# When a block of the adjacency matrix may be stored: an exact count of slots in place of a constant

## The reference

```
h = relu(layernorm(x)); x = x + L0(h)   # three rounds of: tmp = tmp + segment_sum(tmp[src], dst) / deg
h = relu(layernorm(x)); x = x + L1(h)   # means of edge attributes by src and by dst, then two dense products
h = relu(layernorm(x)); x = x + L2(h)   # attention over edges: softmax of scores by dst, weighted sum
h = relu(layernorm(x)); x = x + L3(h)   # messages from node features, spherical and radial edge terms, gates
```

## Time and profile before

| | |
|---|---|
| time, median of 3 runs | 2495.79 us (2492.46 to 2499.66) |
| span of the profiled execution, first to last instruction | 2205.5 us |
| the profiled execution's own time | not recorded; the median less the span is 290.3 us |
| mean granted TensorE clock | 0.824 of 2.4 GHz |
| build of the adjacency, DVE's first visit to PE's first step of L0 | 66.35 to 344.29 us |
| visits, pairs, stores | 590, 106, 27 |

### The profile page before, as it was taken

The page is one execution under the profiler, slowest core; times in us unless marked ns, Lnnn a source line. Parts: engine busy times, 40 slices in busy tenths (PEclk is TensorE's granted clock), DMA queues, the critical chain, the costliest instruction groups (busy, mean ns, idle before and its releaser), DMA issues.

```text
span 2205.5 us, 36859 instructions
## 1 busy us (share of the span) xinstructions
PE 1640.1 (74%) x8603; PEld 1281.5 (58%) x8603; DVE 1788.0 (81%) x5309; ACT 1113.4 (50%) x2935; POOL 865.1 (39%) x861
## 2 busy tenths in 40 slices
PE   3656667998998998735678777776657788888876
PEld 2322226887887886524567676676635555555555
DVE  8898887998998995886777877878577877777776
ACT  1766666876886983200234334243544444444443
POOL 2000000000000000077777777773037777777772
PEclk8886668999999999856788888798758878777777
DMA  6355558664765764156666566563112222222221
GB/s 215 108 150 149 155 157 270 245 247 155 268 242 194 267 249 180 34 162 163 168 163 177 163 158 186 161 184 103 48 52 54 55 56 55 55 55 54 56 55 46
DMA packets 192504, 314.88 MB, mean 143 GB/s; under 512 B 25905, under 2 KB 139448, under 8 KB 182450
## 3 DMA queue, kind: packets, MB, share of 16 engines
q1 hardware_dynamic: 163344, 248.12, 34.7%
q0 software_dynamic: 27712, 63.56, 11.3%
q10 hardware_dynamic: 1250, 0.86, 0.2%
HBM read 232.38 MB, written 80.07 MB: 142 GB/s over the span
## 4 chain that ended last, share of the span: by engine, by line
POOL 24%; DVE 13%; PE 13%; issue 12%; DMA 2%; ACT 1%; SPq 1%; DVEq 0%; POOLq 0%; ACTq 0%
POOL G L704 13%; POOL G L689 7%; POOL SCR L689 5%; PE PS L1930 2%; PE PS L2037 2%; DVE HOT_R L1187 2%; PE PS L1931 2%; PE PS L1906 2%; PE PS L1821 1%; DVE GROUPED_R L1202 1%; DVE GROUPED_R L1196 1%; DMA G<-table,src_idx 1%; ACT HB L726 1%; SPq L608 1%; DVE SCR L1362 1%
## 5 line engine op out<-in xcount | busy, mean ns | idle before, releaser
L689 POOL DMA_INDIRECT G<-table,src_idx x252 | 271.2, 1076 | 969.6 <-DMA table<-RX 889.3
L704 POOL DMA_INDIRECT G<-table,gather_idx x415 | 407.4, 982 | 249.4 <-issue 123.7
L2037 PE MATMUL PS<-SCR,OH 128*128 128x256 f32 x830 | 283.0, 506 | 107.7 <-DVE SCR L1660 104.6
L2037 PEld LDWEIGHTS PS<-SCR,OH 128*128 128x128 f32 x830 | 201.6, 252 | 160.6 <-DVE SCR L1660 121.4
L1821 PE MATMUL PS<-ALL_R 128*128 128x256 f32 (+3 forms) x2025 | 267.3, 289 | 21.7 <-DVE ALL_R L1250 9.1
L1906 PE MATMUL PS<-RX,OH 128*128 x830 | 178.4, 370 | 137.3 <-DVE SCR L1362 85.8
L1821 PEld LDWEIGHTS PS<-ALL_R 128*128 128x128 f32 (+1 forms) x2025 | 252.3, 191 | 24.6 <-DVE ALL_R L1250 9.5
L1906 PEld LDWEIGHTS PS<-RX,OH 128*128 128x128 f32 x830 | 148.3, 245 | 168.9 <-issue 163.7
L1930 PE MATMUL PS<-AT 128*128 128x128 f32 x830 | 203.9, 332 | 20.0 <-issue 11.5
L1781 PE MATMUL PS<-HOT_R,GROUPED_R 128*119 128x448 f32 x830 | 194.0, 381 | 24.7 <-DVE G L1208 23.3
L1769 PE MATMUL PS<-AT,G 128*128 128x400 bf16 x474 | 142.8, 450 | 81.1 <-ACT PS L819 51.1
(11 more groups left out here) (395 smaller groups left out, 3425.2 us busy)
## 6 DMA issues: line engine op xcount, KB each, us to landing
ALL_R<-adjacency SPq DMA_DIRECT2D x72, 1600.0 KB, 6.9
adjacency<-ALL_R SPq DMA_DIRECT2D x26, 1600.0 KB, 7.4
AT<-gathered_rows SPq DMA_DIRECT2D x103, 256.0 KB, 3.8
gathered_rows<-G SPq DMA_DIRECT2D x63, 256.0 KB, 2.3
AT<-dst_in_block SPq DMA_DIRECT2D x103, 128.0 KB, 4.0
gathered_rows<-SCR SPq DMA_DIRECT2D x40, 256.0 KB, 2.2
G<-table,gather_idx POOLq DMA_INDIRECT x415, 2.6
G<-table,src_idx POOLq DMA_INDIRECT x252
```

The lines of the kernel that those rows point to most:

```text
L689: pool.indirect_dma_start(score_rows(i)[:, q], None, tables[0], bass.IndirectOffsetOnAxis(ap=src_idx[:, v:v + 1], axis=0)).then_inc(s(f"sc ...
L704: pool.indirect_dma_start(G[:, p, q, :], None, tables[i], bass.IndirectOffsetOnAxis(ap=gather_idx[:, p, q:q + 1], axis=0)).then_inc(s(f"{n ...
L2037: ins = pe.matmul(PS[:, q, 0:MSG], OH[:, p, q, :], view(SCR, M_AT + (p * VB + q) * MSG, [[1, MSG]]), start=True, stop=True)
```

## The change

DVE now works out, ahead of the keys, how many overflow slots begin before the last sub of each block, adds the block's own slots, halves, and leaves one word for each of the 25 blocks beside ACT's words. SP waits once until these are there, then loads a word before each store and waits for that many pairs in place of the constant. The last two stores wait for 106 as before.

```diff
         pair_words = AT[0:1, 17, 0:SLOTS // 2].bitcast(I32)
+        store_words = AT[0:1, 17, 128:128 + NBLK].bitcast(I32)
...
             sp.dma_start(vector_rows, view(AT, (SH + 1) * (NV + 1), [[1, 3 * (NV + 1)]])).then_inc(s("vectors_moved"), 16)
+            sp.wait_ge(s("stores_planned"), 1)
             for b in range(SBLK):
-                sp.wait_ge(s("pair_copied"), min(PER_BLK * (b + 1) + OVER, SLOTS) // 2)
+                copied = sp.value_load(store_words[0:1, b:b + 1], min_val=PER_BLK // 2, max_val=SLOTS // 2) if b < NBLK else SLOTS // 2
+                sp.wait_ge(s("pair_copied"), copied)
...
             dve.memset(small[:, 7, :], 0.0).then_inc(s("words_made"), 1)
+
+            last_sub, in_order, earlier = (HB[0:1, at:at + n] for at, n in ((2640, NBLK), (2680, OVER), (2200, NBLK * OVER)))
+            dve.tensor_scalar(last_sub, iota[0:1, 0:NBLK], float(PER_BLK), float(PER_BLK - 1), ALU.mult, ALU.add)
+            done(dve.tensor_tensor(in_order, jumps[0:1], iota[0:1, 1:1 + OVER], ALU.subtract))
+            done(dve.tensor_tensor(earlier.rearrange("o (b j) -> o b j", b=NBLK), view(HB, 2680, [[0, NBLK], [1, OVER]], 1),
+                                   view(HB, 2640, [[1, NBLK], [0, OVER]], 1), ALU.is_lt))
+            done(dve.tensor_reduce(HB[0:1, 2700:2700 + NBLK], earlier.rearrange("o (b j) -> o b j", b=NBLK), AX, ALU.add))
+            done(dve.scalar_tensor_tensor(HB[0:1, 2730:2730 + NBLK].bitcast(I32), HB[0:1, 2700:2700 + NBLK], 2.0, last_sub, ALU.add, ALU.add))
+            dve.tensor_scalar(store_words, HB[0:1, 2730:2730 + NBLK].bitcast(I32), 1, None, ALU.arith_shift_right).then_inc(s("stores_planned"), 1)
```

## The result

The changed kernel took 2479.29 us (median of 5 runs, 2472.43 to 2484.47), the kernel before 2499.66 us in the same timing (5 runs, 2492.46 to 2503.45): ratio 0.9911, 95% interval 0.9882 to 0.9940, or 15 to 29 us less. A ratio is an estimate from all runs of a timing and differs a little from the quotient of the two medians: by the ratios the three differences are 22, 33 and 30 us, by the medians 20, 31 and 24. So the kernel is faster in each timing, by 20 to 33 us, and the build, as its traces show, is 31 us shorter.

The account below looks back on a forecast made before the run. The build was taken to be bound by a store-landing loop of 10.55 us a block against DVE's 8.76. DVE's end moving -28.4 us plus 0 added work gave 2495.8 - 28 = 2468 us, range 2460 to 2481 for 8 in 10.

Parts of the forecast that it names:

- my own case: Whole execution: DVE's last visit at 302.5, time 2468 us within its own range 2463 to 2474; chance 0.64.
- the rival of the slow loads: Adjacency build: nearly all ACT and PE register loads slow, 10.08 us a block, -10 to -14 us, 2482 to 2486; chance 0.14.
- The loop: Build from block 3: store, landing, next copy, next store take 10.55 us a block against DVE's 8.76; one pair earlier just suffices.
- What is late next: Build after the change: last visit between DVE's floor, 298.5, and three slow loads a block, 306.8; 302.5 taken.
- the first rival: Build: DVE's floor is reached, loads cost nothing beyond slack, -32.4 us, 2463; chance 0.12.
- My case of two slow loads in a block: ACT's pairs in the build: two slow register loads of four make 8.88 us a block, practically DVE's pace; last visit 298.5.
- The sum: DVE's last visit moves from 330.94 to 302.5, -28.4 us; PE's first step moves to 315.9 and the shift reaches the end whole.
- What lies around the span: Outside the profiled span: 290.3 us between it and the median of the runs, taken as unchanged.
- What it adds: Six DVE instructions, 1.8 us, covered by idle times of 6.35 and 3.37 us; 25 SP loads off the path: 0 us.
- Step 5: L0: PE's wait before step 5, 6.93 us, stays, as its first fetch leaves at 362.60 and flies as long as before.
- Nothing gained: Build: PE's 68.5 us for cleared banks is a limit of eight banks, pace stays 10.55, 2494 to 2496; chance 0.06.
- The clock: PE: the denser build carries its low clock, 0.67, into L0, 1.6 us more a step; 25 steps give 2508; chance 0.04.

Follow-up runs that it names:

- experiment 1: The kernel before, unchanged, profiled and timed again beside the others: 2197.89 us, ratio 0.9998, span 2205.4.
- experiment 2: The changed kernel, unchanged, timed again on the same chip as the kernel before: 2167.30 us against 2197.78, ratio 0.9848.
- experiment 3: The kernel before with the exact pair counts written as constants, no plan on DVE and no register loads on SP: 2167.42 us, ratio 0.9841.
- Experiment 4: The changed kernel with its plan and register loads, but each store also waits for the old constant: 2196.73 us, ratio 0.9990.
- Experiment 5: The kernel before with its store constants less one pair for blocks 0 to 21: 2473.98 us against 2498.08, ratio 0.9884.
- experiment 7: The kernel before and the changed kernel, both unchanged, once more side by side: before 2470.47 us, ratio 1.0015; changed 2437.21 us against 2460.75, ratio 0.9878.

## Why the prediction was right, and where it was off

The time (2479.3) lies in the range of 2460 to 2481 and the direction was right. The step that frees the build was the one named, a wait of which ACT's 24.7 us was the visible part, but which held back all three engines. That the time fell inside the range owes something to luck. It is above the 2463 to 2474 that I gave for my own case and near the rival of the slow loads (2482 to 2486), while the build did the opposite and gained more than I forecast. Had the whole 31 us shown in that timing, the time would have been near 2469; on the chip of experiments 1 to 4, where both kernels are some 300 us quicker, no absolute figure of mine could have been met.

- **The loop.** Right. The first store left at 77 us and the next at 87 (about 78 and 87 were forecast), and the wait for landings is gone. The later stores came every 9.6 us and not every 8.8: before, the constants grew by four pairs a block, but the exact counts grow from 13 to 98 between blocks 2 and 22, by 4.25, since they follow the overflow slots as well. It cost nothing, because the block being copied no longer waits for them. Experiment 5 confirms the step "with four pairs it is 8.76 us, just enough": one pair is the whole gain. Experiment 4 shows that nothing but the moment of the store matters.
- **What is late next.** This is the term of the sum that was mis-sized. I put DVE's last visit at 302.5, between its own floor (298.5) and three slow loads in a block. It ended at 298.53, and PE's first step came at 311.89, both ahead of the 301 to 305 and 314 to 318 that I named as signs: the first rival, with a chance of 0.12, is what happened in the build. That 298.53 is so close to 298.5 is chance, for the visits took 233.7 us and not 232.1, and the first came 1.5 us early. The mechanism behind my margin exists, as the two kernels without source one-hots show (24 us between whole and quarter stores), but its price is 8.67 us a block and not 8.9 to 9.5, under DVE's 8.82. My case of two slow loads in a block was the true one: over 0.6 us take 49 of ACT's 106 loads, in the trace of before and in that of after alike. It is no matter of chance either. In every trace with whole stores two of ACT's four or five loads behind a store are slow (three behind the last one of the series), those that begin about 2 and 4.5 us after it was issued; loads that begin up to 0.4 us after it, or 7.0 us and more, are quick. After the store of 107.33 us in the changed kernel they are these (columns of the earlier trace rows):

```profile
107.33 0.51 SPq L571 DMA_DIRECT2D adjacency<-ALL_R  x1
...
L811 ACTq TENSOR_LOAD <-AT x1: 275/275/275, 107.4 to 107.4; - x1
...
L811 ACTq TENSOR_LOAD <-AT x2: 904/910/917, 109.3 to 111.9; - x2
...
L811 ACTq TENSOR_LOAD <-AT x2: 274/278/283, 114.4 to 116.4; - x2
```

So a store does not slow loads for all of its 7.4 us, as I had it, and stores that come more often make no third load of a block slow. I had leaned toward three because ACT's median after the first store was 0.872 us. The same median of after, 92 to 311, is 0.286. With two kinds of loads in nearly equal number a median lands on either; here it says "about half" both times, and no more.
- **The sum.** -32.4 us from the two first traces against -28.4. Of these, 1.5 us is an earlier first visit (64.84 against 66.35); over the runs it lies between 64.4 and 67.7 whatever the kernel, so it is scatter. From first to last visit it is 264.6 against 233.7 us, -30.9, and the traces of experiments 2, 3, 5 and 7 have 233.7 too. That is the size of the step in the build. The two later timings agree with it (by their intervals -29 to -38 and -20 to -40 us), the first, with -15 to -29, does not quite.
- **What lies around the span.** Wrong. I took 290 us around the span as a fixed part of the execution. The kernel before ran in 2198 us with a span of 2205 us at one time and in 2470 with a span of 2462 at another. Nearly all of the difference lies inside the two gather stages (698 and 569 us, or 828 and 695). It did no harm, since the shift is the same in both, but a reader of the first trace would have missed 290 us of the time that was measured.
- **What it adds.** Right, by rows and by experiments 3 and 4: 1.55 us on DVE (1.8 forecast), hidden behind the two idle times named, and 0.27 us for a load on SP, ahead of a wait. At most the 1 to 1.6 us of experiment 4 stay unexplained.
- **Step 5.** Right: 6.88 us against 6.93.
- **The rivals.** Nothing gained and slow loads taking over: refuted in the build by the first trace after (233.7 us of visits, 49 slow loads of 106). The clock: it rose in the build (0.79 from 140 on, before 0.67) and L0 kept 0.97 in both kernels of experiment 7.

That the first timing shows 22 us (15 to 29) and the two others 33 and 30 is not settled. The build gained its 31 us in that trace too. Experiments 1, 2 and 7 find no stage that gives anything back, on a quick chip and on a slower one, and the interval of experiment 7 (20 to 40 us) overlaps the first one. Scatter of the gathers would do, and is the likely reading, but it was not shown for that timing, which has no trace of before beside it.

## What to carry to other kernels

A wait in a ring of buffers can cost more than its own row says: 24.7 us of waiting for landings stood for 31 us, and the waits of the other engines for each other were its echo. Compare the loop (from release to landing to the next release) with the next engine's own pace; if the loop is longer by less than one unit of work, releasing one unit earlier is the whole gain. A median of two kinds of values says little: count each kind, and look where in the loop it falls. And check that the span of a trace agrees with the times before reading shares from it; where they are 290 us apart, the trace shows another execution than the one that was timed.

## What the runs showed of the hardware

- A register load from SBUF is slow during part of a large store from SBUF: 0.59 us for PE's 8 words, up to 2.10 with whole stores (1600 KB), up to 1.16 behind a quarter store, where the median is 0.592; for ACT's one word 0.27, up to 1.08 with whole stores and up to 0.66 with quarter ones. With whole stores two of ACT's loads behind each store are slow, begun about 2 and 4.5 us after its issue; with quarter stores one, begun 2 us after it.
- While GpSimd adds two tensors in SBUF (6.45 us), a DVE instruction of 0.25 us takes 6.43.
- The gather stages of one and the same kernel took 698 and 569 us in one timing and 828 and 695 in another, on another chip, with GpSimd's busy time for the second stage 406 and 420. Inside the second stage a gather starts every 1.28 us in the quick trace and every 1.58 in the slow one, while the packets on the gathers' queue take 0.12 us on average in both. Whether it goes with the chip or with the occasion, and what delays the gathers, was not looked for and stays open.
